# Layer 0's routed rows in one region per expert: 5 full blocks behind the first four batches, 14 groups behind the rest

## What is computed

```
x = x + g_msa * attention(modulate(ln(x)))          # layers 0, 1, 2
h = modulate(ln(x))
logits = h @ w_gate                                   # layer 0: 4 experts, the top 2 of each token
top_w = softmax over the two chosen logits
y_e = gelu(h @ w1[e] + b1[e]) @ w2[e] + b2[e]
x = x + g_mlp * sum_k top_w[k] * y_{e_k}
x = x + mlp(...)                                      # layers 1, 2
x_rot = x + (z @ expm(A) - z) @ U.T,  z = x @ U       # layer 3, U from the QR of P (288 x 64)
```

## Time and profile before

| | us |
|---|---|
| median of 3 runs | 1294.09 (1289.55 to 1294.12) |
| the profiled execution's own time | 1286.9 |
| its span in the trace | 1285.1 |
| PE busy in the span | 1178.6 (92%) |
| DVE, ACT, POOL busy | 903.0, 740.3, 451.8 |
| mean granted clock of PE | 0.964 of full |

### The profile page before, as it was taken

How to read it: one execution, slowest core, us unless ns; L and a number is a source line. 1 busy time by engine, 2 the same in 40 slices (tenths; PEclk the granted TensorE clock), 3 DMA queues, 4 the chain that set the end, 5 groups by cost and what they waited for, 6 DMA issues and landing times.

```text
span 1285.1 us, 31567 instructions
## 1 busy us (share of the span) xinstructions
PE 1178.6 (92%) x12305; PEld 849.7 (66%) x12305; DVE 903.0 (70%) x2048; ACT 740.3 (58%) x1477; POOL 451.8 (35%) x818
## 2 busy tenths in 40 slices
PE   5778878879999999899999996999999999999998
PEld 3344445538887888677777784776766677576775
DVE  6999988864444333686766568777848979877454
ACT  5675867654454343376564565654657657676643
POOL 4322433642234122733212346242633432342220
PEclk9798979979999999899999997999999999999999
DMA  7697535475678867674455553322112101000002
GB/s 204 177 362 260 184 69 142 154 243 173 236 249 295 252 216 237 228 156 148 109 134 134 159 154 95 47 39 69 28 16 55 20 5 19 10 16 6 11 1 76
DMA packets 105161, 166.73 MB, mean 130 GB/s; under 512 B 42813, under 2 KB 89014, under 8 KB 98358
## 3 DMA queue, kind: packets, MB, share of 16 engines
q1 hardware_dynamic: 101670, 154.46, 42.0%
q0 software_dynamic: 3072, 9.97, 2.3%
q10 hardware_dynamic: 272, 0.29, 0.1%
HBM read 124.88 MB, written 35.34 MB: 125 GB/s over the span
## 4 chain that ended last, share of the span: by engine, by line
PE 73%; DVE 12%; issue 4%; ACT 4%; DMA 3%; POOL 2%; SPq 1%; DVEq 0%; ACTq 0%; POOLq 0%
PE P L1920 17%; PE P L1748 12%; PE P L1930 6%; PE P L1932 6%; PE P L1931 6%; PE P L1877 4%; DVE NM L2188 3%; PE P L1765 2%; PE P L1868 2%; PE P L1775 2%; PE P L1853 2%; PE P L1844 2%; POOL STG L2762 1%; ACT ARENA L2627 1%; PE P L1831 1%
## 5 line engine op out<-in xcount | busy, mean ns | idle before, releaser
L1920 PE MATMUL P<-XT,W 128*128 128x256 f16 x2394 | 278.5, 274 | 6.0 <-ACT W L2519 1.8
L1920 PEld LDWEIGHTS P<-XT,W 128*128 128x128 f16 x2394 | 230.2, 98 | 45.3 <-issue 10.2
L1930 PE MATMUL P<-W,H 128*128 128x288 f16 x684 | 196.1, 287 | 0.0
L1932 PE MATMUL P<-W,H 128*128 128x288 f16 x684 | 195.6, 286 | 0.0
L1931 PE MATMUL P<-W,H 128*128 128x288 f16 x684 | 195.6, 286 | 0.0
L2660 ACT ACTIVATE G<-P 128x512 f32<-128x512 f32 (+1 forms) x190 | 105.3, 554 | 152.2 <-PE P L1920 132.0
L2188 DVE TENSOR_REDUCE NM<-P 128x2 f16<-128x512 f32 x256 | 159.7, 686 | 16.5 <-PE P L1853 15.9
L2627 ACT ACTIVATE ARENA<-P 128x512 f32<-128x512 f32 x256 | 133.6, 609 | 50.7 <-PE P L1868 48.6
L1748 PE MATMUL P<-WQ,XT 128*128 128x288 f16 x1008 | 141.8, 291 | 6.8 <-issue 3.6
L2362 DVE TENSOR_TENSOR H<-G,H 128x512 f16<-128x512 f32 (+1 forms) x123 | 80.8, 668 | 80.1 <-ACT H L2661 79.7
L1748 PEld LDWEIGHTS P<-WQ,XT 128*128 128x128 f16 x1008 | 95.7, 99 | 41.2 <-issue 12.5
(11 more groups left out here) (384 smaller groups left out, 2266.0 us busy)
## 6 DMA issues: line engine op xcount, KB each, us to landing
W<-scr_w SPq DMA_DIRECT2D x22, 1440.0 KB, 6.5
W<-scr_w SPq DMA_DIRECT2D x22, 1368.0 KB, 6.2
XT<-scr_x SPq DMA_DIRECT2D x22, 320.0 KB, 7.4
scr_w<-W SPq DMA_DIRECT2D x4, 1440.0 KB, 8.6
scr_w<-W SPq DMA_DIRECT2D x4, 1368.0 KB, 9.0
scr_y<-TM SPq DMA_DIRECT2D x35, 144.0 KB, 4.0
scr_x<-XT SPq DMA_DIRECT2D x1, 4160.0 KB, 13.8
H<-in_L_w SPq DMA_DIRECT2D x9, 432.0 KB, 6.8
```

Of the source, the lines that this page charges most:

```text
L1920: ins = e.matmul(bank(st)[:, 256 * k:256 * k + 256], W1[:, w, m * 128:(m + 1) * 128], XT[:, b, x, :], start=i == 0, stop=i == 6)
L1930: e.matmul(o, hi, W2[:, 2 * m, :], start=False, stop=False)
L1932: ins = e.matmul(o, lo, W2[:, 2 * m, :], start=False, stop=m == 8)
```

## The change

All of layer 0 gets one region of DRAM, in which each expert has 9 blocks of 256 rows (`BLOCKS`), 36 in all; a token's place in its expert's part is counted on over both pieces. The pieces are now batches 0 to 3 and 4 to 7. Behind the first route, 5 groups are run (`EARLY` = 2 x 4 - 4 + 1): with 8 groups' worth of rows over 4 experts at least 5 blocks are full. Behind the second, the other 14, so 19 = 2 x 8 + 3 in place of 22. Which block a group takes is now known only at run time, so `gi_in` and `y_out` read a register as well, and `g_which` works it out (20 or 21 small DVE operations in place of 4; `g_slots` has 8 in place of 12). Each expert's last block is filled out with harmless rows by `pad` (4 register reads and 4 DMAs of 320 KB) instead of filling all of `scr_x` ahead (`x_init`: two DMAs of 320 KB in place of 7040 KB), and `scr_y` is now cleared ahead by `y_init`, four DMAs of 2592 KB. `gather` becomes one generator over all 8 batches that waits for the last group of all. The first weighing of a result row moves from DVE to ACT (`mix_one`). `SPLIT` parts layer 1's first pair of batches in the MLP, `TIMES` is 9 in place of 14, and the Householder steps are dealt behind another step.

```diff
-PIECES = ((0,1,2,3,4),(5,6,7))
-GROUPS = tuple(2 * len(p) + NE - 1 for p in PIECES)
+PIECES = ((0,1,2,3),(4,5,6,7))
+EARLY = 2 * len(PIECES[0]) - NE + 1
+GROUPS = (EARLY, 2 * B + NE - 1 - EARLY)
+SLOTS = (PIECES[0], PIECES[1] + PIECES[0])
+BLOCKS = B + 1
-SPLIT = {(2, 3): [(0,), (1,)]}
-TIMES = 14
+SPLIT = {(1, 0): [(0,), (1,)], (2, 3): [(0,), (1,)]}
+TIMES = 9
...
+        def y_start(e):
+            y0.append(do(sp, "y_init", 0.8, incs=16, e=e, src=[blank, saved[1, e], saved[2, e]]))
...
-            s = do(dve, "g_slots", 2.4, raises="g_top", incs=12, p=p, j=j, src=m, mask=mask)
+            s = do(dve, "g_slots", 1.4, raises="g_top", incs=8, p=p, j=j, src=m, mask=mask)
+            e = do(dve, "g_which", 2.2, raises="g_top", incs=20 if p else 21, p=p, src=s)
-            e = do(dve, "g_which", 0.6, raises="g_top", incs=4, p=p, src=s)
...
+            if p:
+                tok["sent", p] = [sent, tok["sent", 0], do(sp, "pad", 3.0, incs=16 * NE, src=[started, e])]
...
-        def gather(p):
-            while ("y", p) not in tok:
+        def gather():
+            while ("y", 1) not in tok:
                 yield "wait"
-            for b in PIECES[p]:
+            for b in range(B):
+                p = 0 if b in PIECES[0] else 1
...
-                    y = do(dve, "mixed", 1.1, incs=3, i=i, n=n, t=t, k=k, src=got[n], rows=rows, w=tok["wab", p])
+                    h = do(act, "mix_one", 0.42, i=i, n=n, t=t, src=got[n], w=tok["wab", p])
+                    y = do(dve, "mixed", 1.12, incs=2, i=i, n=n, t=t, k=k, src=h, rows=rows, w=tok["wab", p])
...
         def householder():
-            while ("wab",1) not in tok:
+            while ("route",1) not in tok:
...
+            def pad(st):
+                q.wait_ge(st["src"])
+                for k in range(NE):
+                    row = e.value_load(PADI[0:1, k:k + 1], min_val=0, max_val=256 * (BLOCKS * NE - 1))
+                    e.dma_start(scr_x[bass.ds(row, 256), :], scr_b).then_inc(st.sem, 16)
...
             def gi_in(st):
-                at = 256 * st["g"]
-                q.wait_ge(st["free"], st["src"])
-                e.dma_start(HL[st["b"]], scr_x[st["p"]][at:at + 256, :].rearrange("(n p) c -> p n c", n=2)).then_inc(st.sem, 16)
+                q.wait_ge(st["free"], st["src"], st["which"])
+                block = block_of(st["p"], st["g"])
+                e.dma_start(HL[st["b"]], scr_x.rearrange("(k n p) c -> k p n c", n=2, p=128)[bass.ds(block, 1)].rearrange("a p n c -> p (a n) c")).then_inc(st.sem, 16)
...
             def y_out(st):
-                at = 128 * st["at"]
-                q.wait_ge(st["src"])
-                e.dma_start(scr_y[st["p"]][at:at + 128, :], TM[st["k"]][:, :]).then_inc(st.sem, 16)
+                q.wait_ge(st["src"], st["at"], st["which"])
+                block = block_of(*st["key"])
+                e.dma_start(scr_y.rearrange("(k n p) c -> n p k c", n=2, p=128)[st["n"], :, bass.ds(block, 1), :], TM[st["k"]][:, :].unsqueeze(1)).then_inc(st.sem, 16)
```

More of the change, by code:

```diff
@@ L25 @@
 LAT, FILL, TAB = 0.08, 0.15, 1.3
-SIZES = dict(x_in=295, w_in=442, cond_in=345, w2_in=442, w_back=1400, w_keep=1400, g1_in=147, g2_in=295, tv_in=295, tv_out=295, out=295, rows_in=295, x_init=3000, sent=164, got=295, gi_in=328, y_out=147, gm_in=147, v_in=640, wp1_in=350, p_in=74, hh_row=37)
+SIZES = dict(x_in=295, w_in=442, cond_in=345, w2_in=442, w_back=1400, w_keep=1400, g1_in=147, g2_in=295, tv_in=295, tv_out=295, out=295, rows_in=295, x_init=640, y_init=2650, pad=1300, sent=164, got=295, gi_in=328, y_out=147, gm_in=147, v_in=640, wp1_in=350, p_in=74, hh_row=37)
 AHEAD = 3
-X_AFTER = 0
-PIECES = ((0,1,2,3,4),(5,6,7))
-GROUPS = tuple(2 * len(p) + NE - 1 for p in PIECES)
+PIECES = ((0,1,2,3),(4,5,6,7))
[3 more added lines that the diff above has]
+BLOCKS = B + 1
 ROW = 640
@@ L307, in run, with program @@
         pass
[L310 removed]
+def program(nc, I, out, scr_ada, scr_v, scr_o, scr_w1, scr_w2, scr_x, scr_y, scr_b):
     ctx = ExitStack()
@@ L856, in feed @@
                 yield "wait"
-            n = len(PIECES[p])
             for g in range(GROUPS[p]):
-                b = PIECES[p][g % n]
-                while g >= n and ("upped", p, g - n) not in tok:
+                b = SLOTS[p][g % len(SLOTS[p])]
+                while b in user and ("upped", *user[b]) not in tok:
                     yield "wait"
-                ld = do(sp, "gi_in", 0.1, raises=f"x_in{b}", incs=16, p=p, g=g, b=b, free=TR[2 * b] + TR[2 * b + 1], src=tok["sent", p])
+                user[b] = p, g
+                ld = do(sp, "gi_in", 0.6, raises=f"x_in{b}", incs=16, p=p, g=g, b=b, free=TR[2 * b] + TR[2 * b + 1], src=tok["sent", p], which=tok["route", p])
                 yield
@@ L884, in gather @@
                 i, _, free = rSTG.take()
-                got = [do(pool, "got", 2.6, raises=f"got{i}_{n}", incs=32, p=p, i=i, n=n, t=2 * b + n, free=free, src=tok["y", p], w=tok["wab", p]) for n in range(2)]
+                got = [do(pool, "got", 2.1, raises=f"got{i}_{n}", incs=32, i=i, n=n, t=2 * b + n, free=free, src=tok["y", 1], w=tok["wab", p]) for n in range(2)]
                 yield got
@@ new lines, in g_which @@
+                q.wait_ge(st.at(12))
+                e.tensor_reduce(bi, cd, AX.X, ALU.add).then_inc(st.sem)
+                e.tensor_copy(EGI[:, at:at + n], ef).then_inc(st.sem)
+                q.wait_ge(st.at(13))
+                e.scalar_tensor_tensor(out=bi, in0=bi, scalar=FE[:, 0:1], in1=g, op0=ALU.add, op1=ALU.add).then_inc(st.sem)
+                q.wait_ge(st.at(15))
+                e.tensor_tensor(bi, bi, uu, ALU.max).then_inc(st.sem)
+                q.wait_ge(st.at(16))
+                e.tensor_scalar(bi, bi, float(B), None, ALU.min).then_inc(st.sem)
@@ new lines, in g_which @@
+                q.wait_ge(st.at(17))
+                e.scalar_tensor_tensor(out=bi, in0=ef, scalar=float(BLOCKS), in1=bi, op0=ALU.mult, op1=ALU.add).then_inc(st.sem)
+                q.wait_ge(st.at(18))
+                e.tensor_copy(BLI[:, at:at + n], bi).then_inc(st.sem)
+                if p == 0:
+                    e.tensor_scalar(G0, G0, float(EARLY), None, ALU.min).then_inc(st.sem)
+                    q.wait_ge(st.at(20))
+                    e.scalar_tensor_tensor(out=FE, in0=GE, scalar=float(EARLY), in1=G0, op0=ALU.min, op1=ALU.subtract).then_inc(st.sem)
+                else:
+                    e.tensor_copy(PADI[:, :], EBN).then_inc(st.sem)
@@ L2981, in out_ @@
                 e.dma_start(out_v[:, 2 * b:2 * b + 2, :], OUT[st["i"]]).then_inc(st.sem, 16)
-            work = dict(hh_row=hh_row, c_in=cin, x_in=x_in, p_in=pin, cond_in=cond_in, cond_out=cond_out, w_in=w_in, w2_in=w2_in, w_keep=w_keep, w_back=w_back, x_init=x_init, rows_in=rows_in, gi_in=gi_in, y_out=y_out, gm_in=gm_in, g1_in=g1_in,
+            work = dict(hh_row=hh_row, c_in=cin, x_in=x_in, p_in=pin, cond_in=cond_in, cond_out=cond_out, w_in=w_in, w2_in=w2_in, w_keep=w_keep, w_back=w_back, x_init=x_init, y_init=y_init, pad=pad, rows_in=rows_in, gi_in=gi_in, y_out=y_out, gm_in=gm_in, g1_in=g1_in,
                         g2_in=g2_in, top_row=top_row, wp1_in=wp1_in, tv_out=tv_out, tv_in=tv_in, t_row=t_row, v_in=v_in, u_dup=u_dup, out=out_)
@@ L2986, in _ @@
                 work[st.kind](st)
-            for name in ("out0", "out1", "out2", "os0", "os1", "tv_out", "w1_keep", "w2_keep", "x_init", "sent0", "sent1", "tm0", "tm1", "tm2", "tm3"):
+            for name in ("out0", "out1", "out2", "os0", "os1", "tv_out", "w1_keep", "w2_keep", "x_init", "y_init", "pad", *(f"sent{p}" for p in range(len(PIECES))), "tm0", "tm1", "tm2", "tm3"):
                 e.wait_ge(sems[name], counts[name])
```

122 lines of the change are left out of this document (75 added, 47 removed).

## The result

The kernel after took 1307.8 us (median of 4) against 1292.8 for the kernel before: ratio 1.0134, 95% interval 1.0108 to 1.0161. It is 1.3% slower where 2.3% faster was forecast. On a second chip, where before takes 1311, the same file stood at 1.0023 (1.0001 to 1.0046). So the ratio of two kernels differed by a per cent between two chips.

What follows compares the result with a forecast made beforehand. Behind 291.6 us nearly every removed matmul was taken as time gained, with DVE setting the earlier pace. 1286.9 - 43.7 + 0 + 35 - 20 - 1 = 1257.2, plus 7.2 for the median: 1264 us, range 1246 to 1286.

Steps and rivals of the forecast that it cites:

- Three groups, -43.7: Layer 0's expert groups: 387 fewer matmuls on PE, all taken as time gained, -43.7 us.
- SP's reads and the early stage, 0 and 0: Added register reads cost 0; ahead of the first group DVE's earlier finish and PE's moved work cancel, 0.
- The reloads, 0: Weight reloads among groups: SP's reads stand ahead of writes, not between a group's last matmul and its reload; 0.
- PE idle under 5 among groups: Sign of being right: layer 0's groups in steps of 14.6 to 15 us, PE idle under 5.
- rival of late reloads: SP's reads push W1 and W2 reloads out of cover: +21, 1285, or 1278 with half; chance 0.10.
- The new end of layer 0: Layer 0's end to layer 1's first up: 24 idle in the gap and 11 in the bare attention, +35 us.
- less cover later: Layers 1 and 2: attentions have 8 groups fewer beside them; allowed -1 to +8, taken as -1.
- - 20: Removed at layer 1's start and behind 756.7: waits of 6.0 and 12.0 us and 2.3 of slow clock.
- the 18 of removed waits: PE waits that go: 6.0 us before layer 1's first batch and 12.0 behind layer 0's last group.
- the 58: Layer 1's first qkv to first up, without groups: 58 us for some 47 of PE work, slow clock included.
- The rule on interleaving: Layer 1's first batches: kernels with several regimes may gain by interleaving; by it, unmixing is a loss, counted as +35.
- The rival with the slow clock: Bare stretch at layer 1's start: PE's 47 us run at 1.2 GHz throughout, 94 for 58, +36, 1300; chance 0.04.

Runs made afterwards that it cites:

- two splits: SPLIT of after, layer 1's first pair of batches parted too: added to before 1.0223; after itself 1.0134 and 1.0023; 22 groups in after's scheme 1.0386.
- LAT 0.09: Planner cost LAT at 0.09 in place of 0.08: before 0.9935, after 0.9925, before with the gather behind layer 0's last group 1.0259, 19 groups gathering after 11 0.9747.
- the late gather: Before with the gather of all eight batches behind layer 0's last group: 1.0472 with its one split, 1.0159 with after's split, 1.0259 with LAT 0.09.
- one split: Before's SPLIT, layer 1's first pair not parted: after 0.9904 (9 turns) and 0.9882 (14), 22 groups in after's scheme 1.047, before with late gather 1.0472.
- the kernel without reads: After with constant addresses for group loads, output stores and the four padding writes, so SP reads no register for an address of layer 0's rows: 1.0022.
- The LAT pair: Before with LAT at 0.09, 0.9935, and the same with the gather of all batches behind layer 0's last group, 1.0259.
- the early gather: After with second-phase blocks ordered so the first four batches' gather may start after 11 groups, with before's SPLIT and TIMES: 0.9727; with LAT 0.09: 0.9747.
- FILL: Planner cost FILL at 0.17 in place of 0.15: before 1.0022, after 0.9916.

## Why the prediction was wrong

First the two profiles of before and after, by the stages of the earlier trace rows and of the windows above; all figures are us of PE, busy or idle.

| term | forecast | measured |
|---|---|---|
| busy, whole span | -43.7 - 2.3 | -27.1 |
| idle up to the first group | 0 | +5.0 |
| idle from there to the last group (20.6, was 10.5) | -6.0 | +10.1 |
| idle at the end of layer 0 and start of layer 1 (32.7, was 12.6) | +35 - 12 | +20.2 |
| idle in the rest (25.6, was 12.7) | -1 | +12.9 |
| span | -30 | +21.2 |

(The idle time of a stage is its length less PE's busy time.) So the 51 us between forecast and result are 19 in busy time, 16 among the groups, 14 in the rest, 5 in the early stage and -3 at the new end.

**Three groups, -43.7: right in size.** Busy time times the mean granted clock is an estimate of PE's work at full clock: 1178.6 x 0.964 = 1136 before and 1151.5 x 0.951 = 1095 after, 41 less. The work went; the lower clock made the rest of it longer. By the runs, 22 to 19 groups is 47 us with two splits (1.0386 to 1.0023). With LAT 0.09, from the late gather in before to the kernel after, all else of the change included and on two chips, it is 3.3%, 43 us. With one split it is 75; each such pair carries a draw.

**SP's reads and the early stage, 0 and 0: right.** Without the address reads: 1.0022 for 1.0023. The first up came at 268.4 (265 forecast), with 5 us more idle time ahead of it.

**The reloads, 0: failed, but not by the reads.** "PE idle under 5 among groups" came out at 20.6, and 17.4 of it are waits for W<-scr_w, the sign that the prediction named for its rival of late reloads. Since after and the kernel without reads idle there for 18.0 us each on the second chip, it is not the reads. The late-gather kernels of before's scheme idle there for 8.5 to 12.7 us. One wait of 8.3 us looked like the cause in one profile and was 1.2 in the next; what makes the reloads late stays open.

**The new end of layer 0 and less cover later, +35 - 20 - 1 = +14: this sum failed, by the clock and the cover.** The late gather alone costs 61, -8 and 42 us (4.7%, -0.6%, 3.2%), 32 in the mean of three draws that spread widely. The LAT pair is the cleanest, since both its first groups start within 3 us, but its two profiles are from two chips. The windows of before with LAT 0.09, by stage: to the first group; groups and layer 1's first attention; gap; to the next up; rest.

```profile
0.00:272.80 272.80, 207.51 (x2157) 124.15 (x2158) 238.70 (x523) 184.78 (x340) 100.31 (x155) 0.91 0.61 191
272.80:754.00 481.20, 462.98 (x4985) 361.55 (x4983) 270.17 (x667) 234.99 (x493) 149.01 (x321) 0.99 0.68 200
754.00:778.00 24.00, 16.86 (x165) 13.63 (x163) 21.11 (x47) 10.44 (x19) 20.54 (x25) 0.80 0.50 121
778.00:785.00 7.00, 6.91 (x41) 4.79 (x42) 5.30 (x14) 4.00 (x9) 5.58 (x13) 0.70 0.26 89
785.00:1275.90 490.90, 480.57 (x4965) 344.22 (x4963) 367.85 (x817) 313.93 (x614) 162.28 (x303) 1.00 0.16 30
```

The same with the late gather:

```profile
0.00:275.40 275.40, 206.87 (x2167) 124.26 (x2168) 239.47 (x526) 183.97 (x338) 98.99 (x156) 0.93 0.60 187
275.40:625.00 349.60, 341.10 (x3120) 278.20 (x3118) 132.65 (x353) 139.37 (x314) 79.36 (x169) 1.00 0.77 252
625.00:661.40 36.40, 21.52 (x364) 19.02 (x359) 23.96 (x54) 6.73 (x17) 24.78 (x42) 0.58 0.34 72
661.40:730.00 68.60, 54.46 (x754) 37.06 (x756) 60.48 (x137) 41.82 (x81) 39.90 (x67) 0.88 0.49 91
730.00:1322.00 592.00, 566.64 (x5915) 400.53 (x5914) 433.66 (x973) 385.52 (x743) 193.32 (x388) 0.98 0.18 31
```

PE idles for 7.2 of the 31 us between the last group and layer 1's next up in the first, and for 29.0 of 105.0 in the second: +21.8, where I had 35 less the 18 of removed waits. That was about right, and partly by luck. In after the gap has ten steps of the exponential with 320 matmuls, where I counted 160 and 5.7 us; PE was busy there for 20.4 us and idle for 11.7, not 24. The bare stretch behind it idled for 21.0, not 11. The two errors cancel: 32.7 for 35.

Two terms did not come right. *Less cover later*, taken at -1 of -1 to +8: the rest idles for 25.4 us in place of 10.3, **+15** (the groups idle 9.7 less, the early stage 3.2 more). And *the clock*: the same 12305 matmuls are busy for 1190.6 us in place of 1174.8, **+16**, with the granted clock at 0.58 in the gap and 0.88 behind it; I had "put it into the 58". Nor is it all at the gap: the 592 us behind the next up ran at 0.98, where before's last 491 had 1.00. Idle time and the slow clock beside it must be priced apart. The sum is 30.3 idle and 15.8 busy, the 46 between the spans. The pair of before and after says the same: +12.9 idle in the rest, and busy time 19 over the forecast.

The 58 was, as feared, too low too: 74.5 in after, 68.6 to 85.6 in every kernel with the late gather. Unmixing layer 1's first batches from the groups costs 42 us by the LAT pair. Mixing them again in the 19 groups gives 20 us with one split (0.9882 to 0.9727, one chip) and 23 with LAT 0.09 (0.9925 to 0.9747, two chips). The rule on interleaving that I weighed (the Trainium skill, Perfetto Trace Analysis, Optimization Strategy) pointed the right way. The rival with the slow clock, at 0.04, came in part: in the fourteen profiles with the late gather the stretch ran at a granted clock of 0.79 to 0.88 and the gap ahead of it at 0.56 to 0.63, so at 1.2 GHz for most of the gap.

The rule of bursts that start at half clock (the Trainium skill, TensorE: Matmul & The Clock Gate, HAM oscillation) agrees with the trace for the 42 qkv behind the gap, 6.98 us in place of 5.31. It does not cover the gap itself, where the clock fell while PE waited for only 0.8 to 0.9 us between steps, nor the stretch as a whole.

**The order, no term at all: the step that was missing.** I counted `SPLIT` only as a help for cover. It makes the planner find another order: 1.2% of after's time, 2.2% of before's. With like edits on both sides the changed kernel is faster in three of four pairs: 1.1% (FILL), 1.1% (one split) and 2.0% (two). In the fourth (LAT, 0.9925 and 0.9935) the two are the same within their intervals. Only as the two files stand is it slower, by 0.2 or 1.3%. So the sign of the result is, by these draws, that of the order found and of the chip. That the gain is small is the change's own, as far as so few draws tell: 43 to 47 us won with three groups, 32 to 42 given back by the late gather. What makes a given order bad was not found, and the chip's part (1.1% on the same file) stays open.

The gain can be had. The 19 groups with the early gather took 0.973 and 0.975 of before, in two draws on two chips, less than any other kernel of the table.

## What to carry to other kernels

When work is removed by making a later stage wait for all of an earlier one, price the lost overlap as three things: the gap, the idle time that comes back in the stages that lost their partner, and the slow clock in and behind the gap. Where a planner or a scheduler sets the order, an edit is also a redraw: change one harmless constant in both kernels first, and see how wide their times spread, before a per cent or two is put down to the edit. And a wait seen in one profile is no cause until another execution shows it too.

## What the runs showed of the hardware

- The same file on two chips: before 1292.8 and 1311 to 1314 us (1.4%), after 1307.8 and 1314.6 (0.5%). Two programs need not slow down alike.
- 32 float32 matmuls of 64 x 64 went from 1.20 to 2.03 us in the middle of a chain that had waited only 0.9 us between them: the clock fell all the same, to a mean of 0.63 over the gap.
- 61 register reads less on SP (19 loads, 38 stores, 4 paddings), priced at 0.77 us each, changed the time by nothing that these runs can tell (1.0022 for 1.0023).
- The same reload, in the same order of operations, kept PE waiting for 11.2 us in one execution and 2.2 in another.
